# A graph network's block-pair sums: two packed words per register load, and counts and weights copied out together

## The reference, cut to what matters

```python
x = x + gat(relu(layernorm(x)), edges)            # 4 heads of 64, softmax over incoming edges
x = x + filtered_sum(relu(layernorm(x)), edge_attr, edges)
x = x + gated(relu(layernorm(x)), edge_weight, edge_weight_n2, edges)
x = x + gat_and_mlp(relu(layernorm(x)), edges)
```

```python
counts[s, d]     = sum over edges (s, d) of 1
weights_in[s, d] = sum over edges (s, d) of edge_weight
```

## Time and profile before

| | |
|---|---|
| runs | 6443.0 us median; 6439.95, 6443.0 and 6450.62 |
| span of the profiled execution | 6438.6 us |
| busy: TensorE, VectorE, ScalarE, POOL | 4806.3, 4624.4, 2192.1, 2881.2 us |
| first loop (line 1544) | 1513 to 2256 us |
| its matmuls | 2880 |
| second loop (line 1640) | 3520 to 4840 us |
| granted TensorE clock, mean | 0.873 of full speed |
| DMA | 695,981 packets, 1161.93 MB, mean 180 GB/s |

### The profile page before, as it was taken

One profiled execution on the slowest core, in us unless ns is written; L12 is line 12 of the kernel. 1 busy time (PEld: TensorE's weight loads), 2 busy tenths in 40 slices (PEclk: granted clock), 3 DMA queues, 4 the chain that ended last, 5 costly groups with the idle time before them and its releaser, 6 DMA issues.

```text
span 6438.6 us, 83860 instructions
## 1 busy us (share of the span) xinstructions
PE 4806.3 (75%) x23649; PEld 3414.6 (53%) x23649; DVE 4624.4 (72%) x5654; ACT 2192.1 (34%) x4386; POOL 2881.2 (45%) x3112
## 2 busy tenths in 40 slices
PE   7826999985888933477774777777778999974648
PEld 4415888874777823233332666666666555861213
DVE  9796776435877869899997888888885000159796
ACT  5623443333555334355552222222206000133223
POOL 0077777777777777740000777777740000000000
PEclk9999999997999955699996888878878999967777
DMA  9993444436888799832233666666641444126573
GB/s 245 280 225 89 139 139 139 137 125 220 293 288 285 244 339 332 274 116 70 72 74 99 219 215 221 217 216 218 219 112 48 144 154 152 40 73 218 176 227 127
DMA packets 695981, 1161.93 MB, mean 180 GB/s; under 512 B 268057, under 2 KB 483586, under 8 KB 681701
## 3 DMA queue, kind: packets, MB, share of 16 engines
q1 hardware_dynamic: 327403, 534.90, 28.6%
q0 software_dynamic: 134656, 328.87, 16.4%
q10 hardware_dynamic: 233594, 293.96, 13.1%
HBM read 672.47 MB, written 484.93 MB: 180 GB/s over the span
## 4 chain that ended last, share of the span: by engine, by line
DVE 30%; PE 29%; POOL 18%; issue 12%; DMA 6%; ACTq 2%; ACT 1%; SPq 1%; DVEq 0%; POOLq 0%
POOL slots_by_block_pair L953 13%; PE psall L1695 8%; PE psall L1544 8%; DVE arena L2253 6%; DVE arena L2263 6%; DVE arena L2224 6%; DMA arena<-table_x,arena 4%; PE psall L1628 4%; POOL arena L986 4%; DVE arena L2317 3%; DVE arena L2460 3%; ACTq L1132 2%; POOL idle L955 1%; PE psall L1402 1%; DMA arena<-counts 1%
## 5 line engine op out<-in xcount | busy, mean ns | idle before, releaser
L986 POOL DMA_INDIRECT arena<-table_x,arena x856 | 952.1, 1112 | 992.8 <-DMA arena<-slots_by_src 687.7
L953 POOL DMA_INDIRECT slots_by_block_pair<-arena x806 | 828.2, 1028 | 574.4 <-DVE arena L2009 315.1
L1605 PE MATMUL psall<-arena 128*65 128x313 f32 (+1 forms) x2800 | 868.1, 453 | 262.2 <-DVE arena L2263 262.2
L975 POOL DMA_INDIRECT slots_by_src<-arena,pos_s x806 | 838.4, 1040 | 253.3 <-issue 236.2
L1628 PE MATMUL psall<-arena 128*125 128x256 f32 x1712 | 579.3, 511 | 342.8 <-DVE arena L2317 342.8
L1143 ACT ACTIVATE arena<-psall 128x250 f32<-128x250 f32 (+2 forms) x1002 | 327.1, 368 | 1440.0 <-PE psall L1640 1043.3
L1544 PE MATMUL psall<-arena 128*128 128x250 f32 x2880 | 655.1, 388 | 164.1 <-DVE arena L2204 78.3
L1605 PEld LDWEIGHTS psall<-arena 128*65 128x65 f32 (+1 forms) x2800 | 337.4, 130 | 791.9 <-DVE arena L2263 403.8
L1511 PE MATMUL psall<-shared_w,arena 128*128 128x256 f32 x3264 | 750.3, 383 | 1.7 <-DVE arena L2158 1.7
L1544 PEld LDWEIGHTS psall<-arena 128*128 128x128 f32 x2880 | 557.1, 196 | 262.6 <-issue 194.4
L1628 PEld LDWEIGHTS psall<-arena 128*125 128x125 f32 x1712 | 439.5, 263 | 459.4 <-DVE arena L2317 362.8
(11 more groups left out here) (326 smaller groups left out, 7223.6 us busy)
## 6 DMA issues: line engine op xcount, KB each, us to landing
arena<-slots_by_src SPq DMA_DIRECT2D x107, 1040.0 KB
filters<-arena ACTq DMA_DIRECT2D x204, 520.0 KB, 2.7
arena<-filters POOLq DMA_DIRECT2D x202, 520.0 KB, 5.5
slots_by_src<-shared_on SPq DMA_DIRECT2D x8, 9230.0 KB, 77.3
weights_out<-arena ACTq DMA_DIRECT2D x125, 320.0 KB, 3.1
arena<-counts SPq DMA_DIRECT2D x50, 781.5 KB, 4.4
counts<-arena ACTq DMA_DIRECT2D x125, 312.5 KB
weights_in<-arena ACTq DMA_DIRECT2D x125, 312.5 KB
```

Of the source, the lines that this page charges most:

```text
L953: G.indirect_dma_start(slots_c, bass.IndirectOffsetOnAxis(ap=pos_c[:, j, q:q + 1], axis=0), rec_c[:, c, :], None).then_inc(s["scattered_c" ...
L975: G.indirect_dma_start(slots_s, bass.IndirectOffsetOnAxis(ap=pos_s[:, c:c + 1], axis=0), ring_s[:, g % SLOTS, c % TG, :], None).then_inc(r ...
L986: G.indirect_dma_start(hg[:, f % 2, j, :], None, t_x1, bass.IndirectOffsetOnAxis(ap=pay_s[:, f % 2, j, S_IDX:S_IDX + 1].bitcast(I32), axis ...
L1605: last = MM(ps[gat_bank(n, wn, h_, c)][0:F + 1, 0:z - a], rows, g["e1"][:, q % g["RE"], a:z], start=(b == 0), stop=(b == NT - 1))
```

## The change

- `ends_i` has 156 words (`LASTS` = 625 // 4) and not 625. A word holds two numbers of 11 bits each: the last tiles of pairs of blocks 4k+1 and 4k+3, the only ones that the loop asks for. VectorE packs them in two operations where one stood.
- `sums_out` loads 2 words at every fourth `m` and takes a number out with a shift and a mask. This holds for both loops.
- Counts and weights of a pair of blocks lie side by side in one staging tile, `stage_both`. One instruction copies both for two pairs, 500 elements in each of 128 partitions. The two stores read every other 125 columns of it, so what one DMA reads in a partition is five runs of 500 B with gaps between them.
- The spare columns of `diag` are filled with zeros. Addresses of some tiles move.

```diff
+LASTS = NB // 4
-        d_last = dram("last_tiles", (1, NB), I32)
+        d_last = dram("last_tiles", (1, LASTS), I32)
-        stage_c = view(o_stage, LANES, 3 * PAIRS * P).rearrange("p (b k) -> p b k", k=P)
-        ends_i = view(o_ends + NB, 1, NB).bitcast(I32)
+        ends_i = view(o_ends + NB, 1, LASTS).bitcast(I32)
-        stage_in = view(o_ohw + 4 * CT_G * P, LANES, 3 * PAIRS * P).rearrange("p (b k) -> p b k", k=P)
+        o_both = o_ohw + 4 * CT_G * P
+        stage_both = view(o_both, LANES, 3 * PAIRS * 2 * P).rearrange("p (b k) -> p b k", k=2 * P)
...
-                for v, frm in ((v_ct, stage_c), (v_in, stage_in)):
-                    act.dma_start(v[:, blk, to], frm[:, cut, :].rearrange("p b k -> p (b k)")).then_inc(st_c[g % 3], 16)
+                for v, c in ((v_ct, 0), (v_in, P)):
+                    act.dma_start(v[:, blk, to].rearrange("p (b k) -> p b k", k=P), stage_both[:, cut, c:c + P])\
+                        .then_inc(st_c[g % 3], 16)
...
-                    if m % 4 == 0:
-                        _, last_tile = nc.values_load_multi_w_load_instructions(ends_[0:1, a:min(a + 8, NB)],
+                    if m % 4 == 0 and m // 2 < LASTS:
+                        _, last_tile = nc.values_load_multi_w_load_instructions(ends_[0:1, m // 2:m // 2 + 2],
                                                                                 [mybir.EngineType.Activation])
-                    act.wait_ge(mm, last_tile[z - 1 - 8 * (m // 4)] & (2048 - 1) if z < NB else 1 + T1)
+                    act.wait_ge(mm, (last_tile[m // 2 % 2] >> (11 * (m % 2))) & (2048 - 1) if z < NB else 1 + T1)
-                        for to, c, width in parts:
-                            last = A(to[:, u:v, :], sums[:, b:b + v - u, c:c + width], ACT.Copy)
+                        last = A(to[:, u:v, :], sums[:, b:b + v - u, 0:width], ACT.Copy)
...
-                    link(V.tensor_scalar(ends_i, ends_b[0:1, :], 1.0, None, ALU.add))
+                    two = tjunk[0:1, 0:LASTS]
+                    link(V.scalar_tensor_tensor(two, ends_b[0:1, 3:NB:4], 2048.0, ends_b[0:1, 1:NB - 1:4],
+                                                ALU.mult, ALU.add))
+                    link(V.tensor_scalar(ends_i, two, 2049.0, None, ALU.add))
...
+            V.memset(diag[:, P:], 0.0)
```

More of the change, by code:

```diff
@@ L88 @@
 GE_C = TG * SLOTS
+LASTS = NB // 4
+assert 4 * LASTS + 1 == NB and T1 < 2048
 S2_G = -(-EC // TG)
@@ L244, in gnn_kernel @@
         o_stage = o_oh_b + 2 * CT_G * LANES
-        stage_c = view(o_stage, LANES, 3 * PAIRS * P).rearrange("p (b k) -> p b k", k=P)
         o_tab = o_wt + 5 * D + 4 * G3
-        assert o_stage + 3 * PAIRS * P <= o_tab
+        assert o_stage + CT_G * LANES <= o_tab
         tables = view(o_tab, 1, TAB).bitcast(I32)
@@ L251, in gnn_kernel @@
         ends_b = view(o_ends, LANES, NB)
-        ends_i = view(o_ends + NB, 1, NB).bitcast(I32)
[L253 to L257, removed]
+        ends_i = view(o_ends + NB, 1, LASTS).bitcast(I32)
+        tnum = view(o_ends + NB + LASTS, LANES, 12)
+        tcol = view(o_ends + NB + LASTS + 12, LANES, 3 * 12).rearrange("p (n t) -> p n t", n=3)
+        tword = view(o_ends + NB + LASTS + 48, LANES, 4).bitcast(I32)
+        tint = view(o_ends + NB + LASTS + 52, LANES, 12).bitcast(I32).rearrange("p (g j) -> p g j", j=TG)
+        o_diag = o_ends + NB + LASTS + 64
         diag = view(o_diag, LANES, HALF)
@@ L265, in gnn_kernel @@
         o_ohw = o_diag + HALF
-        stage_in = view(o_ohw + 4 * CT_G * P, LANES, 3 * PAIRS * P).rearrange("p (b k) -> p b k", k=P)
-        o_ohs_2 = o_ohw + 4 * CT_G * P + 3 * PAIRS * P
-        assert o_ohs_2 + CT_G * LANES <= o_rec
+        o_both = o_ohw + 4 * CT_G * P
+        stage_both = view(o_both, LANES, 3 * PAIRS * 2 * P).rearrange("p (b k) -> p b k", k=2 * P)
+        assert o_both + 3 * PAIRS * 2 * P <= o_rec
         o_ohw_2 = o_b + 2 * NT * EVEN
@@ L272, in gnn_kernel @@
         ohs = [view(o_, LANES, CT_G * LANES).rearrange("p (j k) -> p j k", j=CT_G)
-               for o_ in (o_oh_b, o_oh_b + CT_G * LANES, o_ohs_2)]
+               for o_ in (o_oh_b, o_oh_b + CT_G * LANES, o_stage)]
         ohw = [view(o_, LANES, 2 * CT_G * P).rearrange("p (j a k) -> p j a k", j=CT_G, a=2)
@@ L313, in gnn_kernel @@
         pay_w = view(o_r1, LANES, T1 * C_REC).rearrange("p (t c) -> p c t", c=C_REC)
-        ends_w = view(o_r1 + T1 * C_REC, 1, NB).bitcast(I32)
-        assert T1 * C_REC + NB <= NT * D
+        ends_w = view(o_r1 + T1 * C_REC, 1, LASTS).bitcast(I32)
+        assert T1 * C_REC + LASTS <= NT * D
         tables_w = view(o_oh + 2 * F_T * P, 1, TAB).bitcast(I32)
@@ L1122, in store_weights, with sums_out @@
                               stage_out[:, PAIRS * (g % 3):PAIRS * (g % 3 + 1), :]).then_inc(st_w[g % 3], 16)
-            def sums_out(ends_, mm, taken, stored_on, each, begin, store, parts):
+            def sums_out(ends_, mm, taken, stored_on, each, begin, store, to, width):
                 twos, stored = -(-NB // 2), 0
@@ L1157, in _ @@
             sums_out(ends_i, s["cb_mm"], s["cb_ev"], st_c, 2, begin_counts, store_counts,
-                     ((stage_c, 0, P), (stage_in, P, P)))
+                     stage_both, 2 * P)
             for h in range(HEADS - 1):
@@ L1249, in _ @@
             sums_out(ends_w, s["wb_mm"], s["wb_ev"], st_w, 1, begin_weights, store_weights,
-                     ((stage_out, 0, LANES),))
+                     stage_out, LANES)
             def agg(it, sl):
```

## The result

The changed kernel takes 6722.8 us (median of 4 runs, 6712.9 to 6727.2) against 6441.5 us before. The ratio is 1.0435, with a 95% interval of 1.0418 to 1.0451. The forecast of 6373 us was wrong in its sign. What happened is the fourth case, which had a chance of 0.08.

What follows compares the result with a forecast made beforehand. The first loop was taken to lose time as TensorE waits for ScalarE's bank fillings, delayed by register loads. -54 - 6 - 15 - 3 + 8 + 0.3 = -70 us gave 6373 us from 6443, range 6335 to 6415.

Steps and rivals of the forecast that it cites:

- the fourth case: First loop, hardware queue 10: stores become the bound above 36 ns a piece; at twice 27 ns +382, 6825 us; chance 0.08.
- Register loads, first loop: ScalarE's 78 loads fall from median 3.17 to 0.9 us, 1.2 behind a store; TensorE's stops behind bank fillings shrink, -54 us.
- the hidden part of the stops: First loop, TensorE: each of 39 stops is really up to 0.16 us longer than the profile measures, -6 us.
- the clock: First loop, TensorE: half the work lost to 1.2 GHz stretches after long stops comes back, -15 us (0 to -33).
- Copies: First loop, ScalarE: one copy of 500 elements at 0.6 us replaces two taking 0.65 us together, -3 us.
- Stores, the issue: ScalarE's queue, first loop: second store of a pair issued in 0.8 us, 50 us more in all, covered by slack.
- Stores, the DMA engines: First loop: 160,000 pieces at 27 ns take 16 engines 270 us, 96% full with the scatter; +8 us on TensorE's register loads.
- POOL's scatter may be slowed without cost: POOL, beside and after the first loop: scatter ends at 2819 us, next gather starts at 3497, so slowing by 100s of us is free.

Runs made afterwards that it cites:

- two-plane kernel: Changed kernel, but its single copy puts counts and weights into two planes, so each store reads 2500 B without a gap: 6347.9 us, ratio 0.9869 against the kernel before.

## Why the prediction was wrong, by its steps

- **Register loads, first loop: right in size, though for half a reason.** Forecast 0.9 to 1.2 us a load and -54 - 6 - 15 us. By themselves they brought -79 us, with loads of 1.32 us in the median. In the loop TensorE's stops behind fillings shrank by 58 us (54 forecast) and its matmuls' busy time by 27.7 (655.1 to 627.4), where 6 + 15 had been put on the hidden part of the stops and on the clock. I had read the difference between 3.17 and 0.556 us as words and company. It was mostly the place of the first word. I saw that 8 words cost six times as much in one loop as in the other and did not ask what differed between the tables.
- **Copies: nothing** (1.0004), where -3 us were forecast. 0.589 us was the forecast duration.
- **Stores, the issue: too dear in the forecast.** The second of a pair is issued in 0.61 us (median), not 0.8.
- **Stores, the DMA engines: the step that failed.** It reads: "A 512 B piece to memory costs [...] 27 ns in the second loop, so 160,000 take 16 engines 270 us", and "The engines have carried more". Both halves rest on rows of another kind. The 27 ns come from pieces that start at multiples of 512 B (`weights_out` has 128 columns a block), the 500 B pieces of the heavy stretch 2310:2640 were reads of `counts` (22 DMAs of 1562.5 KB), and queue 10 wrote `masks` beside them, so that its 75,791 packets hold 711 B each in the mean and not 500. The change writes 500 B at multiples of 500 B, of which only one in eight starts at a multiple of 32 B. That costs 48 ns in the loop, 56 with the scatter away and 61 by itself. 160,000 x 48 ns / 16 are 480 us and not 270. Queue 0 went up too, from 55.3 to 58.8%, over a longer time.
- **The fourth case had the mechanism and the right scale, and too small a chance.** Its threshold was 36 ns a piece, its loop 1125 us against 1036. Its cause, a read beside each write, is not what these runs show: pieces of the same 500 B cost 30 ns once they started well. The Trainium skill ("DMA: Bandwidth & Descriptors", Specifications) names a length, 512 B, below which a transfer is read, modified and written. Here 500 B and even 448 B and 256 B pieces were cheap at a good start, and 512 and 1024 B pieces dear at a bad one; the measurement decides for the start. The same page (How a descriptor splits into AXI transactions) says that a transaction "must start from a 256B-aligned address", and that a piece which does not start there fetches bytes it does not use. It says this of reads. Worked out from its account, which counts in beats of 32 B, a 512 B piece would take 16 beats from a good start, 17 from 4 B behind it and 18 from 64 B behind it (an estimate from that page). The runs show 29, 57 to 73 and 34 ns: the start counts, as there, but the doubling at 4 B is not explained by it.
- **POOL's scatter may be slowed without cost: right.** It ended at 2853 us. The second loop began 273 us later than before, by as much as the end of the first had moved, so nothing waited for it.

Open: why only some of the pieces at a bad start are slow, why the surcharge is as large at 1536 B as at 512 (14 us a series) and all but gone at 2048 B, and why DMAs with one piece in each partition don't pay it. And in the second loop loads of 2 words took 0.50 us but 4 words 0.32: the runs show it as a matter of the place and the number of words, not how the load works.

## What to carry to other kernels

Before you let one copy do the work of two, look at what the stores behind it will write: many short runs to memory (up to 1536 B here) are cheap when each starts at a multiple of 32 B, better of 256 B, and cost up to two or three times as much when they don't. Or keep the runs long: the two-plane kernel has the single copy and its stores of 2500 B, whose price was the same (105 and 106 ns) at both starts tried. Take a price only from a row of the same direction and the same starts; a share of 96% worked out from other rows is no room to spare. And where the same instruction costs six times as much in two places, ask first where its operands lie.

## What was not expected of the hardware

- A write of 512 B that starts 4 B behind a multiple of 512 B takes 57 to 73 ns of an engine in the mean, one at the multiple 29, if many are under way at once; a read of 500 B at any multiple of 4 B takes 31.
- 8 words into registers take 0.55 us from a place at a multiple of 4 words and about 1.8 us at best from one that is 1 or 2 words behind it; 4 words at a good place 0.32 us, 2 words 0.50.
- A store's landing, not its issue, is what a three-deep staging ring must cover: in the changed kernel up to 9.3 us were missing.
